# A 17x17 depthwise convolution cut into cells, a normalisation without GpSimd, and weight loads moved to another queue

## The reference

```
h   = bn1(x)                                      # per channel: x * scale + shift
h   = depthwise conv 17x17, padding 8             # the padding is zero after bn1
h   = gelu(bn2(einsum('bchw,dc->bdhw', h, pw)))
a   = sigmoid(relu(mean_hw(h) @ se_w1.T + b1) @ se_w2.T + b2)
x   = x + gamma * h * a                           # layer 0
xn  = (x - mean_c(x)) * rsqrt(var_c(x) + 1e-5) * ln_g + ln_b
out = mamba(xn) + flip(mamba(flip(xn)))           # layer 1: selective scan over 4096 tokens,
                                                  # 192 channels, 16 states, both directions
```

## Time and profile before

| what | value |
|---|---|
| median of 3 runs | 5832.53 us (5831.49 to 5834.44) |
| profiled execution, its own time | 5829.49 us |
| its span, first to last instruction | 5827.7 us |
| busy PE, DVE, ACT, POOL (share of the span) | 80%, 90%, 55%, 85% |
| HBM traffic | 837 MB read, 212 MB written |
| mean granted TensorE clock | 0.762 |

### The profile page before, as it was taken

The page is one execution under the profiler, slowest core; times in us unless marked ns, Lnnn a source line. Parts: engine busy times, 40 slices in busy tenths (PEclk is TensorE's granted clock), DMA queues, the critical chain, the costliest instruction groups (busy, mean ns, idle before and its releaser), DMA issues. The chain is left out here.

```text
span 5827.7 us, 75897 instructions
## 1 busy us (share of the span) xinstructions
PE 4650.6 (80%) x18020; PEld 1373.6 (24%) x18020; DVE 5252.6 (90%) x3583; ACT 3228.2 (55%) x5273; POOL 4950.5 (85%) x2349
## 2 busy tenths in 40 slices
PE   7998766777787888878787878888778788778887
PEld 5775311111111111111111111111111111111111
DVE  3323658999999999999999999999999999999998
ACT  1223755555555565655655555656556555655664
POOL 0000248999999999999999999999999999999998
PEclk9998886666777777777777777777777777777777
DMA  1001655555665666566666656666666666566566
GB/s 36 25 29 48 198 161 186 185 188 186 207 196 196 205 196 197 196 196 199 199 200 207 198 196 203 201 194 199 195 198 198 201 203 205 192 200 205 189 201 200
DMA packets 363220, 1050.78 MB, mean 180 GB/s; under 512 B 70868, under 2 KB 120294, under 8 KB 312604
## 3 DMA queue, kind: packets, MB, share of 16 engines
q1 hardware_dynamic: 354972, 1034.97, 55.2%
q10 hardware_dynamic: 8064, 14.16, 0.7%
HBM read 837.23 MB, written 211.63 MB: 180 GB/s over the span
## 5 line engine op out<-in xcount | busy, mean ns | idle before, releaser
L1405 POOL TENSOR_TENSOR hc<-hring,c_rep 128x1024 f32<-128x1024 f32 x1541 | 3601.3, 2361 | 70.4 <-DVE hring L1360 67.1
L1360 DVE TENSOR_TENSOR_SCAN hring<-decay,carry,u_ps 128x1024 f32<-128x1024 f32 x1221 | 2820.2, 2331 | 0.0
L1111 PE MATMUL u_ps<-stack_b,w_spread 48*128 48x512 bf16 x2442 | 993.6, 495 | 1005.4 <-DVE hring L1360 1001.5
L1342 DVE TENSOR_TENSOR u_ps<-u_ps,u_rep 128x1024 f32<-128x1024 f32 x1221 | 1473.6, 1207 | 70.7 <-DMA u_rep<-u_scr 55.7
L1236 ACT ACTIVATE decay<-dt_rep,w_a 128x1024 f32<-128x1024 f32 x1222 | 1396.3, 1145 | 219.7 <-DVE hring L1360 207.2
L1129 PE MATMUL y_ps<-hc,w_gather 128*32 128x512 f32 x6144 | 1131.1, 818 | 0.0
L1236 ACT ACTIVATE u_ps<-dt_rep,w_a 128x1024 f32<-128x1024 f32 x322 | 359.2, 1116 | 1102.7 <-DVE hring L1360 1102.4
L1392 POOL TENSOR_TENSOR drive_p<-u_rep,b_rep 128x1024 f32<-128x1024 f32 x322 | 760.6, 2362 | 10.1 <-DMA u_rep<-u_scr 10.1
L1360 DVE TENSOR_TENSOR_SCAN hring<-u_ps,carry,drive_p 128x1024 f32<-128x1024 f32 x321 | 750.7, 2339 | 0.0
L1111 PEld LDWEIGHTS u_ps<-stack_b,w_spread 48*128 48x128 bf16 x2442 | 144.8, 100 | 2367.1 <-DVE hring L1360 2163.1
L684 POOL TENSOR_TENSOR xs<-xc_ln,rs 96x512 f32<-96x512 f32 x64 | 91.4, 1428 | 701.7 <-ACT rs L668 681.4
(11 more groups left out here) (128 smaller groups left out, 4323.2 us busy)
## 6 DMA issues: line engine op xcount, KB each, us to landing
dt_rep<-dt_scr SPq DMA_DIRECT2D x194, 1024.0 KB, 5.9
u_rep<-u_scr SPq DMA_DIRECT2D x194, 1024.0 KB, 7.8
c_rep<-bc_scr SPq DMA_DIRECT2D x260, 512.0 KB, 4.7
b_rep<-bc_scr SPq DMA_DIRECT2D x130, 512.0 KB, 4.3
xn<-xn_scr SPq DMA_DIRECT2D x132, 384.0 KB, 5.1
y_scr<-y_sb SPq DMA_DIRECT2D x768, 64.0 KB, 2.0
xn<-xn_scr SPq DMA_DIRECT2D x132, 256.0 KB, 4.7
dt_scr<-dt_sb SPq DMA_DIRECT2D x260, 128.0 KB, 2.1
```

Of the source, the lines that this page charges most:

```text
L1111: mm = nc.tensor.matmul(u_ps[nv % NSLOT][:, sl], w["spread"][:, q, :], upper(stack_b[drv][:, sl]), start=True, stop=True)
L1342: nc.vector.tensor_tensor(slot[:, :], slot[:, :], u_rep[r][:, b, :], ALU.mult).then_inc(drive_ready, 1)
L1360: nc.vector.tensor_tensor_scan(hring[nv % NHR][:, ::step], factor[:, ::step], term[:, ::step], carry[:, drv, nv:nv + 1], ALU.mult, ALU.add ...
L1405: nc.gpsimd.tensor_tensor(hc[nv % NHC][:, :], hring[nv % NHR][:, :], c_rep[q][:, :], ALU.mult).then_inc(c_applied, 1)
```

## The change

**Convolution.** The image is cut into cells of 16 rows by 4 columns. A matmul now has 64 outputs (the pixels of a cell). Its 128 inputs are 32 rows (16 and 8 above and below) by 4 columns. Five neighbouring cells in x (`CELLS`) cover the 17 columns, so there are 5 steps instead of 9. The four rows of cells are split: two go to PSUM partitions 0-63 (q=0), two to 64-127 (q=1), each a matmul of 2 x 8 x 16 = 256 columns. A batch has 4 x 5 x 2 = 40 matmuls. The matrices need 16 rows x 2 halves = 32 small matmuls a batch, each with a 64-column stationary and 80 moving columns, and 4 copies, all on ScalarE, which also takes all 4 result copies. GpSimd cuts the bfloat16 filter parts for each batch (`take`), and the constants are laid out by new VectorE instructions at the start.

The rows of x are loaded into 64 partitions (column parity x 32 rows) for each of the four rows of cells, so overlapping rows are loaded more than once: 8 DMAs a batch, 240 rows of 4 KB. bn1 then takes 24 VectorE instructions a batch, each on 64 partitions, with 128 or 256 elements a partition, reading every second float.

```
-                sp.dma_start(xraw[par][:, :, :, :], xk[:, bass.ds(ch, CB), :, :])   # one load, 128 partitions
+                rows = d["x_cols"].rearrange("(a y) c b x -> a y (c b x)", a=2)
+                def put(p, q, a, lo, n):
+                    sp.dma_start(xraw[buf][p:p + n, q, :], rows[a, lo:lo + n, cols]).then_inc(x_in[buf], 16)
+                put(PAD, 0, 0, 0, ROWS)                       # PAD = 8, ROWS = 32, NCY = 4
+                put(ROWS + PAD, 0, 1, 0, 2 * PAD)
+                put(ROWS + 3 * PAD, 0, 1, 2 * PAD, PAD)
+                for q in range(1, NCY - 1):
+                    lo = q * CY - PAD
+                    sp.dma_start(xraw[buf][:, q, :], rows[:, lo:lo + ROWS, cols]).then_inc(x_in[buf], 16)
+                put(0, NCY - 1, 0, H - ROWS + PAD, 2 * PAD)
+                put(2 * PAD, NCY - 1, 0, H - PAD, PAD)
+                put(ROWS - PAD, NCY - 1, 1, H - ROWS, ROWS)
...
+                    for c in range(CB):
+                        for h in range(2):
+                            for k, cells in enumerate((slice(0, 1), slice(1, NCY - 1), slice(NCY - 1, NCY))):
+                                nc.vector.tensor_scalar(xpad[buf][rows, c, cells, :, NEAR:NEAR + XC], src[:, cells, c, :, h::2],
+                                                        scale[...], shift[...], ALU.mult, ALU.add)
...
-                            for k in range(SHIFTS):
-                                last = nc.tensor.matmul(pc[c][:, 0:B * XH]...,
-                                                        toep[par][:, n0:n0 + 2, :]..., xpad[par][:, c, :, k:k + XH], ...)
+                            for k in range(CELLS):
+                                for q in range(2):
+                                    last = nc.tensor.matmul(pc[c][64 * q:64 * q + 64, 0:B * XH]...,
+                                                            toep[par][:, c * CELLS + k, :],
+                                                            xpad[par][:, c, q::2, :, k:k + XC], ...)
+                                if k == 2:
+                                    weights(s + 1, 1 - par, c)
```

```
-                for dst, src in mixer.loads:
-                    sp.dma_start(dst, src).then_inc(w_loaded, 16)
+            @block.gpsimd
+            def _(pool):
+                for dst, src in mixer.loads:
+                    pool.dma_start(dst, src).then_inc(w_loaded, 16)
...
-                    nc.scalar.activation(act_out[b % 2][:, :, 8 * col:8 * col + 8].rearrange("c y x -> c x y"), ...
+                    nc.scalar.activation(act_out[b % 2][:, 32 * f:32 * f + 32, 16 * x:16 * x + 16].rearrange("c y (r o) -> c r y o", o=CX), ...
```

```
+                nc.vector.tensor_tensor(centrer[:, :], one[:, :], averager[:, :], ALU.subtract)
...
+                    nc.vector.scalar_tensor_tensor(xs[:, r, :], px[s % NX][0:C, :], lng[:, 0:1], rs[:, r, :], ALU.mult, ALU.mult)
...
+                    nc.vector.tensor_scalar(xo[:, r, :], xs[:, r, :], lng[:, 1:2], None, ALU.add)
-                over_slices(dve, (4, add), (3, centre), (0, gain))
+                over_slices(dve, (5, add), (1, scale), (0, shift))
-                over_slices(pe, (2, mean), (0, variance))
+                over_slices(pe, (3, centre), (1, variance))
-                over_slices(act, (4, square), (3, invert), (0, store))
+                over_slices(act, (4, square), (2, invert), (0, store))
-                    nc.gpsimd.tensor_tensor(xs[:, r, :], xc[:, r, :], rs[:, r, :], ALU.mult).then_inc(scaled, 1)
```

More of the change, by code:

```diff
@@ L127, in convolution @@
         band_f = sb("band_f", [3 * FROWS, 2 * (2 * H - 1)])
[L128 to L132, removed]
+        wide = sb("wide", [3 * FROWS, 2, (C + 2 * CB) * CELL])
+        part = [sb(f"part{i}", [3 * FROWS, 2, CB * CELL], BF16) for i in range(2)]
+        bands = sb("bands", [3 * FROWS, CY, 2, ROWS], BF16)
+        toep = [sb(f"toep{i}", [P, CB * CELLS, CY * CX]) for i in range(2)]
+        xraw = [sb(f"xraw{i}", [2 * ROWS, NCY, CB * B * XH]) for i in range(2)]
+        xpad = [sb(f"xpad{i}", [P, CB, NCY, B, XP]) for i in range(2)]
         bnp = sb("bnp", [P, 4, C])
         bnt = sb("bnt", [P, 3, C])
-        scale = sb("scale", [P, C])
-        shift = sb("shift", [P, C])
+        inside = sb("inside", [P, 2])
+        scale = sb("scale", [P, 3, C])
+        shift = sb("shift", [P, 3, C])
         eps = sb("eps", [P, 1])
@@ L153, in convolution @@
         h_evac = [sem(f"h_evac{i}") for i in range(CB)]
-        xk = d["x_cols"]
         NCONST = 3 + 3 + 4
-        after = [range(NYG // CB * i, NYG // CB * (i + 1)) for i in range(CB)]
+        X_DMAS = 2 + 2 * 3
         with nc.Block() as block:
@@ L175, in _ @@
                         sp.wait_ge(x_ready, 2 * i + par + 1)
-                        sp.dma_start(xraw[par][:, :, :, :], xk[:, bass.ds(ch, CB), :, :]).then_inc(x_in[par], 16)
+                        load(par, ch * (B * XH))
                 for i in range(2):
[L178 to L183, removed]
+                    sp.wait_ge(x_in[i], 16 * X_DMAS * (BATCHES // 2 + 1))
             @block.gpsimd
@@ L202, in evacuate_conv @@
[L202 to L211, removed]
-                    for par in range(2):
[L213 to L221, removed]
+                    nc.gpsimd.memset(xraw[i][:, 0, :], 0.0)
@@ new lines, in _, with take @@
+                    last = nc.gpsimd.memset(xraw[i][:, NCY - 1, :], 0.0)
+                last.then_inc(raw_zero, 1)
+                for i in range(2):
+                    nc.gpsimd.memset(xpad[i][:, :, :, :, 0:NEAR], 0.0)
+                    last = nc.gpsimd.memset(xpad[i][:, :, :, :, NEAR + XC:XP], 0.0)
+                last.then_inc(pads_zero, 1)
+                pool.wait_ge(wide_ready, 5)
+                def take(s, buf):
+                    nc.gpsimd.tensor_copy(part[buf][:, :, :], upper3(wide[:, :, bass.ds(s * (CB * CELL), CB * CELL)])).then_inc(part_ready, 1)
@@ new lines, in _ @@
+                for yg in range(NYG):
+                    evacuate_weights(0, 0, yg, None)
+                with act.Fori(0, BATCHES // 2) as i:
+                    for par in range(2):
+                        s = 2 * i + par
+                        for c in range(CB):
+                            evacuate_weights(s + 1, 1 - par, c, i + par)
+                            act.wait_ge(conv_done[par], CB * i + c + 1)
+                            nc.scalar.copy(hs[:, bass.ds((CB * s + c) * B * XH, B * XH)], pc[c][:, 0:B * XH]).then_inc(h_evac[c], 1)
@@ L241, in _ @@
+                for y in range(CY):
+                    last = nc.vector.tensor_copy(bands[:, y, :, :], band[:, :, H - 1 - PAD - y:H - 1 - PAD - y + ROWS])
+                last.then_inc(band_ready, 1)
                 dve.wait_ge(filt_step, 1)
@@ L538, in normalise @@
     RING = 8
-    NM = 4
+    NX = 4
     with ExitStack() as ctx:
```

202 lines of the change are left out of this document (117 added, 85 removed).

## The result

The changed kernel takes 5624.16 us (median of four runs, 5622.07 to 5625.59) against 5832.99 for the kernel before on the same chip (5831.49 to 5834.44): a ratio of 0.9642, 95% interval 0.9625 to 0.9658. Its profiled execution took 5622.07 us with a span of 5620.2. The forecast was 5595, with a range of 5530 to 5650: the sign and the order of the parts came out, and 29 us of the gain did not. The measured time lies inside that range.

A forecast was written before the change was run, and what follows sets the result against it. TensorE bounds the convolution before, x loads after; the unedited scan is carried over. Gains of 174 (convolution), 39 (pointwise) and 24 (normalise) sum to 237 off 5829.5, giving 5592.5, plus 3.0 for the median: 5595 us, range 5530 to 5650.

The forecast's parts named there:

- the loads of x are the new bound: Convolution: two DMA engines carry the big x loads, setting the batch period; stage 174 us less.
- rival (1): Convolution: x loads spread over 16 engines, TensorE sets 10.4 us a batch; 49 us below forecast, 5546; chance 0.17.
- at 24 GB/s for one engine that is 12.3 us: Convolution: the two busiest DMA engines carry 295 KB a batch, so a load ends every 12.3 us.
- TensorE's 10.4 us a batch: Convolution: halves run side by side, 20 pairs x 0.427 = 8.5 us, plus 1.9 for 32 small matmuls.
- rival (4): Convolution: halves run one after another, weight loads hidden, 19.0 us a batch; 157 us more, 5752; chance 0.05.
- VectorE's 6.6 us: Convolution, bn1: 16 x 0.24 + 8 x 0.345 = 6.6 us a batch, hidden below the period.
- rival (2): Convolution: VectorE becomes the bound, strided halves up to 0.6 us, 14.4 a batch; 52 us more, 5647; chance 0.09.
- transposes 0.43 and matmul 0.43 on TensorE: Pointwise: TensorE's price per group, from which 0.95 us a group was taken; stage 39 us less, 21 at 1.30.
- the mixer loads are hidden: Pointwise: GpSimd's loads at 1.0 us each take 62 us, before VectorE needs them at 74.
- normalise, 24 us forecast: Normalise: GpSimd goes, 2.2 us a slice (2.14 to 2.45), stage 159 instead of 183.3 us.
- The scan: Last stage, scan and output: not edited, carried over at 5005.5 us; forecast wrong if it moves over 10 us.
- (5): Convolution: halves in sequence, each record awaiting its weight load, 29.9 us a batch; 417 us more, 6012; chance 0.02.

The follow-up runs named there:

- Experiment 1: Changed kernel with each of the two big x loads of a batch issued as two, one per parity, 32 rows outermost: 5535.8 us.
- Experiment 9: Experiment 1 plus Experiment 8, with each 34-row filter load issued as 32 rows and 2 rows: 5526.7 us.
- Experiment 8: Changed kernel without the two surplus batches of x loaded after the last used one, and without VectorE's unused batch: 5617.4 us.
- experiment 2: Experiment 1 with the two halves of a channel not alternated, five matmuls of q=0 and then five of q=1: 5661.9 us.
- experiment 5: Changed kernel with pointwise matmul reading only upper halves of its operands (bfloat16) and GELU's old writes, single floats 256 bytes apart: 5615.5 us.
- experiment 6: Changed kernel with the 62 mixer loads back on SP's queue, ahead of the stores, instead of on GpSimd: 5644.4 us.
- experiment 3: Changed kernel with GELU writing in its old form, single floats 256 bytes apart, pixels in another order: 5628.1 us.
- Experiment 7: Kernel before with only the new normalise function: 5800.3 us, ratio 0.9948.

## Why the prediction came out as it did

**Right: the loads of x are the new bound.** The forecast took it from one row of the kernel before, the share of 0.13 while 34-row pieces were under way. Experiment 1 shows it: without the two-engine form the 88 us come, and rival (1)'s time, 5546, is 10 us from the 5535.8 measured. That nearness is partly luck: a batch took 9.5 us and not 10.4, and pointwise gave 22 us and not 39. Experiment 9 shows the same for the filter.
The Trainium skill (DMA: Bandwidth & Descriptors, "Why a DMA increments its semaphore by 16 and not by 1") gives the rule that 34 and 2 both lead to two engines and 32 to 16; these runs agree at all three counts (share 0.13 for 34, 0.12 to 0.14 for 2, 0.91 in experiment 9 while pieces of 32 are under way).

**Mis-sized: "at 24 GB/s for one engine that is 12.3 us".** It measured 13.0 us, 295 KB / 13.0 = 22.7 GB/s. The 24 holds while the two engines are alone (49 to 57 GB/s together, 207 to 211 us), not across a period: around the bursts of the other pieces the windows show 41 GB/s. The first landing came at 33.3 instead of 31. VectorE was ready at 28.9 (28.65 + 0.27, its last constant) and not at 32 to 33, which the landing hid. 25 x 0.7 + 2.3 = 19.8 us is the 19 that the convolution lacks. Experiment 8 confirms that the end of the stage was counted rightly, with the last landing.

**Right, with smaller sizes: TensorE's 10.4 us a batch** measured 9.45 (5 pairs x 0.427 = 2.13 a channel, and 0.23 for eight small matmuls, half of their upper end). Pairing is shown by experiment 2; rival (4)'s price was right for matmuls that never overlap, too high for that order. VectorE's 6.6 us measured 7.46 for 24 instructions, 0.31 each where I had 0.275. The trace tells the two causes apart. An instruction of 256 elements that reads every second float (on 64 partitions) takes no longer than one that read them in a row before (on 128):

```profile
L259 DVE TENSOR_SCALAR xpad<-xraw,scale,shift 128x256 f32<-128x256 f32 x100 | 34.4, 406 | 0.1
L322 DVE TENSOR_SCALAR xpad<-xraw,scale,shift 64x128 f32<-64x128 f32 x400 | 134.9, 337 | 140.9 <-DMA xraw<-in_x_cols 138.1
L322 DVE TENSOR_SCALAR xpad<-xraw,scale,shift 64x256 f32<-64x256 f32 x200 | 80.3, 401 | 0.0
```

The first row is of the kernel before, the other two of the changed one. From one start to the next it is 0.32 us in both for 256 elements. So the stride of rival (2) costs nothing here, and the short instructions, at 0.26 or 0.35 us from start to start instead of 0.24, are what was priced too low. The 7.46 us are hidden by the 13.0, and in experiment 1 by TensorE's 9.5.

**Wrong: "transposes 0.43 and matmul 0.43 on TensorE", so "I take 0.95 us a group".** This is the step that failed, and it contradicts the prediction's own first part, where one float32 matmul of 512 columns has 0.85 us. The 0.43 is one of its two records. The kernel before shows it too:

```profile
530.47 0.60 PE L451 MATMUL pt<-ident,hs 128*96 128x128 f32 x4
530.91 1.02 PE L445 MATMUL pp<-ht,wpw 96*96 96x512 f32 x2
531.77 0.60 PE L451 MATMUL pt<-ident,hs 128*96 128x128 f32 x4
```

531.77 - 530.91 = 0.86. TensorE had 0.86 + 0.44 = 1.30 us a group, exactly the period, before the change. I had named ScalarE since GELU's mean of 1.232 lay near 1.30; experiment 5 shows its true price was 1.08. The prediction did give the right number for this case, 21 us at 1.30 a group, as a bound. The stage gave 22.3, of which experiment 6 makes 20 the removed stall, and experiment 3 about 1 GELU's edit. That GELU's instruction falls to 0.8 us was right (1.244 in experiment 3, 0.776 in the changed kernel), but it brought next to no time here, so the 22 us speak neither for nor against what the prediction says of GELU's writes; only the instruction's own time does.

**Right: the mixer loads are hidden.** I took 1.0 us each with 0.6 to 1.9 as bounds; 0.52 is just under them, and they are issued 32 us into the stage, not 62.

**Right: normalise, 24 us forecast, 27.4 measured.** The first addition came 5.8 us in (467.06 - 461.24), where 6 were counted. A slice took 2.14 us, the lower bound, where 2.2 were taken, and 64 x 0.06 = 3.8 us is the difference. The DMA share in the middle of the stage was 0.88. Experiment 7 shows that it stands by itself.

**The scan** moved by 2.5 us of 5005.5, inside the 10 that were set as the mark.

None of the rivals happened in the changed kernel. In (5), the price from which the 237 us are used up is (339.5 + 237 - 39.4) / 24 = 22.4 us a batch and not 21.8; nothing else hangs on it. The two large errors, 19 us in the convolution and 17 in pointwise, lay on the same side. Each was a price taken from a row that did not show the whole operation. That the sum still came within 29 us owes nothing to the pointwise step, whose mechanism was wrong: the 39 us had a lower bound of 21 at the old period, and that is what happened.

## What to carry to other kernels

In these runs the outermost count of a transfer went with how many DMA engines carried it (34 and 2: two of 16; 32: a share of 0.91), so read the DMA share while only that transfer is in flight; 0.13 in a quiet stretch is worth more than the GB/s of a full one, and the cure may be to issue one transfer as two. Take what an instruction costs an engine from the distance between starts in a stretch without waits, not from its mean duration, and count all records of a float32 matmul. Before calling an engine the bound of a loop, write the starts of all engines for one round side by side and see which of them has no gap.

## What the runs showed of the hardware that I had not expected

- The time of an issue depends on what is in flight: the last constant took SP 2.04 us to issue behind 34-row filter pieces on two engines and 0.43 us behind the spread ones (experiment 9). That full queues are the reason is my reading; no run varies them alone. The issues of x inside the loop were not slow: 0.28 to 0.57 us each, eight of them from 196.46 to 200.71.
- Loads issued by GpSimd took 0.52 us each from start to start (62 from 358.94 to 390.53), hardly more than SP's 0.43 to 0.6.
- ScalarE instructions overlap with their followers: GELU is 1.24 us long and 1.08 us apart (experiment 5). It is not its summed output alone: in the kernel before a square of 0.63 us starts at 729.45 and the next instruction 0.54 us later:

```profile
729.99 0.67 ACT L665 ACTIVATE ln<-pv,ln_eps 96x512 f32<-96x512 f32 x1
```

- A VectorE instruction that reads every second float of SBUF was no slower than one that reads them in a row: 401 against 406 ns for 256 elements a partition.
- TensorE's granted clock went to 0.50 at the end of a gap of 4 us in its work and came back about 3 us later; in the changed kernel the convolution's mean was 0.93, in experiment 1, without gaps, 1.00.
